# Macaron block (gated FFN, window attention, gated FFN): order of the transposes on SP's queue, tokens' split in the first and last blocks, last quarter with hidden units on the partitions

## The chip, the cores and the metric

The kernel runs on one core of a Trainium2 chip. The time is the device time of one execution in microseconds (us); lower is better. Shown are the median of several runs and one profiled execution.

## What is computed

The input x has 8 sequences of 512 tokens with 512 features. Three stages follow each other, each on a layer norm of x and added to x:

```python
x = x + 0.5 * ffn(layernorm(x), w_gate_up, w_proj)
x = x + attention(layernorm(x), Wq, Wk, Wv, Wo)     # 32 heads of 16, window 128
x = x + 0.5 * ffn(layernorm(x), w_gate_up, w_proj)

def ffn(x, w_gate_up, w_proj):                      # hidden width 2048
    gate, up = split(x @ ternary(w_gate_up).T)
    h = silu(gate) * up
    return (h * rsqrt(mean(h * h) + eps)) @ ternary(w_proj).T
```

The ternary weights are made once, at the start: each group of 64 weights becomes -s, 0 or s. In the attention a query sees the keys of its own block of 128 tokens and of the block before it, masked to a distance of at most 128.

## The kernel before

**Tiling.** The 4096 tokens are 32 blocks of 128. Four blocks are a sequence, so the first block of every fourth has no keys before it. A block goes through stream A (first FFN), B (attention) and C (second FFN). An FFN is done in four quarters of 512 hidden units: a gate product and an up product (`up`, line 1054, eight matmuls of 512 columns each), the gating on ScalarE and VectorE (`hid`), a split of the hidden values into an fp16 high and low part (`hh`), a DMA transpose of both parts (`ht`, `hidden_t`, line 449) and a down product of eight matmuls (`down`, line 1100) that adds to a PSUM bank over the four quarters. ScalarE's Square with an accumulator gives each quarter's sum of squares; GpSimd makes 1/rms of them (`root_mean_square`, line 567), and `add_ffn` (line 905) adds the scaled bank to the block. Tokens are normalised (`norm_stats` on VectorE, line 849; `norm_apply` on GpSimd, line 547) into `xhat`, split into high (ScalarE, line 739) and low (GpSimd, line 592) parts `xh`, and transposed by DMA into `xt`. Queries, keys and probabilities are split and transposed in the same way (`qt`, `kt`, `pt`); so is the attention's output (`ot`).

**Order.** All engines walk through the same list of steps, eight per block, and each engine's function `step_of(step)` holds what it does in a step, in written order. Nothing is scheduled dynamically; semaphores connect the engines. Constants place a stage of block b at step 8b + offset: A's quarters at 0 to 3, B's tokens are split at 7, queries, keys and values are projected at 8, 10 and 12, scores run in groups of four heads at 12 to 19, the products with the values two steps later, the output tokens are split at 21, the output projection is at 22, C's tokens are split at 26 and C's quarters run at 28 to 31. So in the middle every step holds an attention group of one block and an FFN quarter of another. In blocks 2 and 3 of A, and in the fourth and third last of C, the quarters are spread over more steps.

**SP's queue** (lines 462 to 520) issues all transfers one after the other and waits in that order. In a step: queries, then keys (a part of four head pairs, then one of twelve, which the scores need two steps later than the first), tokens of B, of the last block of C, of C, of A, output tokens, the probabilities' high and low parts, and last the units:

```python
                s, b, c = ffn_at(step)
                if s:
                    hidden_t(s, b, c, place(step))
                b = complete("C", step, 4)
                if b is not None:
                    sp.wait_ge(d_x3, b + 1)
                    sp.dma_start(of[b * P:(b + 1) * P, :], slot(b)).then_inc(x_out, 16)
```

Behind it come a finished block's store and, at most every eighth step, the load of a new one (`load_x`). TensorE's order in a step is: gate product, scores of two groups (every other step), the down product of two steps before, a product with the values, the up product, then one of the four projections (lines 1202 to 1295).

**The last block** (31) has a written-out path, since its output projection runs at step 271 (`LAST_WO`) in front of the rest: VectorE normalises it and takes the low part (lines 1035 to 1045), ScalarE copies the high part (line 707) and SP transposes it (line 481) in step 272 (`LAST_SPLIT`). Its quarters of C are steps 276 to 279. In its first steps (lines 1114 to 1178) the kernel transposes the raw weights on TensorE in fp32 (`turn`, line 1130) and has a down product of 128 columns a matmul (`down_first`, line 1163).

Of the kernel before, what the change touches and what calls it, by code (L numbers as in the profile page):

```python
# [24 lines left out]
def macaron(nc, x, Wq, Wk, Wv, Wo, w_gate_up, w_proj, out):  # L25
# [52 lines left out]
    LAST_SPLIT = LAST_WO + 1  # L78

    with ExitStack() as ctx:  # L80
# [33 lines left out]
        hid = sb("hid", [P, 2, CH], F32)  # L114
        squares = sb("squares", [P, 2, CH], BF16)
# [67 lines left out]
        h_first = v_flat[:, 0:4096].bitcast(F32).rearrange("p (c d) -> p c d", c=NC)  # L183
        ps_raw = [ps_s, ps_yy]
# [62 lines left out]
        d_hl = {s: sem(f"d_hl_{s}") for s in "AC"}  # L247
        g_sqp = {s: sem(f"g_sqp_{s}") for s in "AC"}
# [12 lines left out]
        NCONST = 10  # L261
# [64 lines left out]

        def projected(step):

            return ps_m if ffn_at(step)[0] else ps_u

# [75 lines left out]
        def _(sp):  # L406
# [55 lines left out]
            for step in range(FIRST_STEP, STEPS + 2):  # L462
                b = block_at(step, Q_AT + 1)
# [5 lines left out]
                b = block_at(step, K_AT + 1)  # L469
                if b is not None:  # L470
                    sp.wait_ge(a_k, b + 1)
                    sp.wait_ge(d_k, b + 1)
                    need(sp, p_s, 16 * (b - 2))
                    for part, pairs in enumerate((slice(0, 4), slice(4, HEADS // 2))):
                        transpose(kt[:, pairs, b % BPS, :],
                                  k4[:, 2 * pairs.start:2 * pairs.stop, :, :].rearrange("p a b c -> p (a b c)"),
                                  t_k[part])
# [46 lines left out]
        def _(pool):  # L524
            pool.memset(id32[:, :], 0.0).then_inc(consts, 1)
            pool.memset(mask[:, :], 0.0).then_inc(consts, 1)
            pool.memset(neg_half[:, :], -0.5).then_inc(consts, 1)
            pool.memset(prob_bias[:, :], PROB_LOG2 * math.log(2.0)).then_inc(consts, 1)
            pool.memset(blocks[:, :], 0.0).then_inc(consts, 1)
            pool.wait_ge(consts, 5)  # L530
# [47 lines left out]

            pool.wait_ge(fs_step, 6)
# [8 lines left out]
            def step_of(step):  # L588
# [14 lines left out]
                for s in "AC":  # L603
                    b = complete(s, step, 1)
                    if b is not None:
                        root_mean_square(s, b)

# [4 lines left out]
        def _(act):  # L612
# [54 lines left out]
            def hidden_hi(s, b, c, n, ready):  # L667
# [8 lines left out]
                act.activation(squares[:, n % 2, :], hid[:, n % 2, :], ACT.Square,  # L676
                               accum_out=sq_quarter[s][:, c:c + 1]).then_inc(a_sq[s], 1)
# [4 lines left out]
            def step_of(step):  # L682
# [24 lines left out]
                if step == LAST_SPLIT:  # L707
                    split_free(act, step, "C")
                    copy(xh[:, 0, :], xhat[:, :], d_xh, 1, a_xl)

# [3 lines left out]

                s, b, c, n = gate_at(step)
                if s:
                    tanh_half(s, b, c, n)

# [16 lines left out]
                for s, offset in SPLITS:  # L735
                    b = block_at(step, offset)
                    if b is not None and in_steps(s, b) and not (s == "B" and b == 0):
                        split_free(act, step, s)
                        copy(xh[:, 0, :], xhat[:, :], g_xh[s], b + 1, a_xh[s])
# [19 lines left out]
        def _(dve):  # L759
# [144 lines left out]

            def add_ffn(s, b, done):
# [50 lines left out]
            def step_of(step):  # L956
# [40 lines left out]
                if b is not None and b > 0:  # L997
# [14 lines left out]

                b = complete("A", step, 2)
# [21 lines left out]
                if step == LAST_WO:  # L1035
# [281 lines left out]
```

## Time and profile before

| | us |
|---|---|
| median of 3 runs (2029.28 to 2033.4) | 2030.42 |
| the profiled execution | 2029.52 |
| its span | 2027.6 |
| TensorE busy in the span | 1889.7 (93%) |
| VectorE busy | 1555.3 (77%) |
| ScalarE busy | 1499.2 (74%) |
| GpSimd busy | 576.8 (28%) |

The rows further down are of this execution. PE is TensorE, PEld its weight loads, DVE VectorE, ACT ScalarE, POOL GpSimd, and SPq the issue of a DMA by SyncE; L1103 is line 1103 of the kernel. A row of a timeline has the start in us, the length in us, the engine, the line, the operation, what is written and read, the tile's shapes, how often (x8: eight in a row, put together), and in brackets how long the engine sat idle before it and what released it. A row of the table by stretch has the stretch, its length and then busy time (and count) of PE, PEld, DVE, ACT and POOL, the granted clock of TensorE as a share of full speed, the mean share in which the core's 16 DMA engines were busy, and GB/s; a table of a single line has the columns PE and PEld alone. A wait row has engine, tile and line that waited, for what, the sum in us, how many times, and the longest. Matmuls are pipelined, so the lengths of single ones overlap.

### The profile page before, as it was taken

The numbers are of one execution on the slowest core, as the hardware profiler recorded it, in microseconds if no ns is written. First come the engines' busy times: TensorE is split into PE (matmuls) and PEld (weight loads), VectorE is DVE, ScalarE is ACT, GpSimd is POOL, SyncE is SP. The second block draws the span as 40 slices with busy tenths as digits, with TensorE's granted clock in tenths as the row PEclk, the third lists the DMA queues.
The fourth block names the chain that finished last, engine by engine and source line by source line (L and its number), as shares of the span: only waits on it lengthen the run. The fifth ranks groups of instructions, "written<-read, shape, count | busy, mean of one in ns | idle before, by whom it ended". The sixth has DMA issues, their size and how long they took to land. (4 is left out here: it accounts for less than half of the span.)

```text
span 2027.6 us, 37731 instructions
## 1 busy us (share of the span) xinstructions
PE 1889.7 (93%) x12447; PEld 913.0 (45%) x12688; DVE 1555.3 (77%) x4079; ACT 1499.2 (74%) x2871; POOL 576.8 (28%) x559
## 2 busy tenths in 40 slices
PE   6677799999999999999999999999999999999777
PEld 3353344444444444444444444444444444444333
DVE  8966787778787888778787878777887878777763
ACT  7836777777876877777876777777777787777762
POOL 2011333322332333222333332233333232222210
PEclk8888999999999999999999999999999999999989
DMA  7334788778986898878886898788887888878862
GB/s 234 121 64 94 140 150 160 135 138 157 156 153 121 146 163 150 141 143 154 156 143 130 149 161 152 142 142 151 158 145 129 150 157 154 146 128 148 140 116 62
DMA packets 1032673, 287.83 MB, mean 142 GB/s; under 512 B 1017120, under 2 KB 1018144, under 8 KB 1031968
## 3 DMA queue, kind: packets, MB, share of 16 engines
q1 hardware_dynamic: 1032480, 285.41, 77.1%
q8 instruction: 102, 1.67, 0.3%
q14 instruction: 91, 0.75, 0.1%
HBM read 25.17 MB, written 8.39 MB: 17 GB/s over the span
## 5 line engine op out<-in xcount | busy, mean ns | idle before, releaser
L731 ACT ACTIVATE masked<-masked,exp_bias,exp_scale 128x256 f32<-128x256 f32 (+1 forms) x1024 | 503.7, 562 | 8.6
L1103 PE MATMUL ps_yy<-wp_t,ht 128*128 128x512 bf16 x1991 | 479.9, 383 | 28.1 <-DMA ht<-hh 26.7
L1058 PE MATMUL ps_gu<-wgu_t,xt_A 128*128 128x512 bf16 x1941 | 469.0, 383 | 16.6 <-DMA xt_A<-xh 3.7
L1058 PE MATMUL ps_gu<-wgu_t,xt_C 128*128 128x512 bf16 x1944 | 463.1, 380 | 11.5 <-DMA xt_C<-xh 3.5
L860 DVE TENSOR_TENSOR prob<-masked,prob 128x1024 f16<-128x1024 f32 (+1 forms) x256 | 287.2, 1122 | 48.0 <-ACT prob L749 47.7
L1103 PEld LDWEIGHTS ps_yy<-wp_t,ht 128*128 128x128 f16 x2016 | 187.6, 98 | 264.9 <-issue 31.9
L554 POOL TENSOR_TENSOR xh<-xhat,xh 128x512 f16<-128x512 f32 x94 | 109.0, 1160 | 691.9 <-ACT xh L615 691.9
L1058 PEld LDWEIGHTS ps_gu<-wgu_t,xt_A 128*128 128x128 f16 x2048 | 192.1, 98 | 230.1 <-issue 11.7
L1058 PEld LDWEIGHTS ps_gu<-wgu_t,xt_C 128*128 128x128 f16 x2048 | 190.7, 97 | 219.9 <-issue 3.9
L875 DVE SCALAR_TENSOR_TENSOR hid<-ps_gu,h_scale_u,hid 128x512 f32<-128x512 f32 x252 | 189.1, 751 | 121.2 <-PE ps_gu L1058 118.4
L615 ACT ACTIVATE hh<-hid 128x512 f16<-128x512 f32 x256 | 160.6, 627 | 152.5 <-DVE hid L875 145.3
L749 ACT ACTIVATE prob<-masked 128x1024 f16<-128x1024 f32 (+1 forms) x256 | 241.2, 942 | 4.2
L869 DVE SCALAR_TENSOR_TENSOR hid<-hid,ps_gu 128x512 f32<-128x512 f32 x256 | 175.1, 684 | 80.6 <-ACT hid L619 80.6
L619 ACT ACTIVATE hid<-ps_gu 128x512 f32<-128x512 f32 x256 | 150.0, 586 | 116.5 <-PE ps_gu L1058 116.2
L726 ACT ACTIVATE exp_bias<-row_max,prob_bias,neg_exp_scale 128x4 f32<-128x4 f32 x256 | 98.2, 384 | 170.0 <-DVE row_max L886 170.0
L860 DVE TENSOR_TENSOR hh<-hid,hh 128x512 f16<-128x512 f32 x256 | 177.7, 694 | 16.1 <-ACT hh L615 15.7
L886 DVE CUSTOM_DVE_ANT_0 masked<-ps_s,mask 128x256 f32<-128x256 f32 (+1 forms) x512 | 168.7, 385 | 9.8 <-PE ps_s L1093 8.2
L676 ACT ACTIVATE squares<-hid 128x512 bf16<-128x512 f32 x256 | 156.9, 613 | 0.0
L1115 PEld LDWEIGHTS ps_om<-v,pt 128*128 128x128 f16 x3584 | 126.4, 96 | 63.9 <-issue 7.3
L1115 PE MATMUL ps_om<-v,pt 128*128 128x33 f16 x3584 | 129.8, 177 | 3.4 <-DMA pt<-prob 3.0
L896 DVE TENSOR_REDUCE o_sum<-ps_om 128x128 f32<-128x256 f32 x128 | 54.2, 424 | 94.9 <-PE ps_om L1115 94.9
L545 POOL TENSOR_TENSOR rstd_B<-var_eps_B,neg_half 128x1 f32<-128x1 f32 x32 | 17.5, 548 | 353.7 <-DVE var_eps_B L855 353.7
(165 smaller groups left out, 2261.6 us busy)
## 6 DMA issues: line engine op xcount, KB each, us to landing
stream<-in_L_attn_x_dram SPq DMA_DIRECT2D x32, 256.0 KB, 3.3
pt<-prob SPq DMA_TRANSPOSE x512, 3.3
out_dram<-stream SPq DMA_DIRECT2D x32, 256.0 KB, 2.4
prob<-in_L_ffn_w_gate_up_dram SPq DMA_DIRECT2D x4, 1024.0 KB, 5.5
ht<-hh SPq DMA_TRANSPOSE x256, 3.2
stream<-in_L_ffn_w_gate_up_dram SPq DMA_DIRECT2D x3, 1024.0 KB, 5.4
stream<-in_L_ffn_w_proj_dram SPq DMA_DIRECT2D x2, 1024.0 KB, 5.2
prob<-in_L_ffn_w_proj_dram SPq DMA_DIRECT2D x2, 1024.0 KB, 4.8
```

The lines of the kernel that those rows point to most:

```text
L615: act.activation(dst, src, ACT.Copy, scale=scale).then_inc(done, 1)
L619: act.activation(hid[:, n % 2, :], ps_g[:, :], ACT.Tanh, scale=0.5 * 2.0 ** -XS_LOG2).then_inc(a_tanh[s], 1)
L676: act.activation(squares[:, n % 2, :], hid[:, n % 2, :], ACT.Square, accum_out=sq_quarter[s][:, c:c + 1]).then_inc(a_sq[s], 1)
L731: t = act.activation(p, p, ACT.Exp, bias=exp_bias[:, 4 * g + h:4 * g + h + 1], scale=exp_scale[:, 0:1])
L749: act.activation(prob_part(prob[:, g % 2, 0, :, :, :], b), prob_f32(b, g), ACT.Copy).then_inc(a_ph, 1)
L860: dve.tensor_tensor(out=dst, in0=src, in1=hi, op=ALU.subtract).then_inc(done, 1)
L869: dve.scalar_tensor_tensor(out=hid[:, n % 2, :], in0=hid[:, n % 2, :], scalar=1.0, in1=ps_g[:, :], op0=ALU.add, op1=ALU.mult).then_inc(d_g ...
L875: dve.scalar_tensor_tensor(out=dst, in0=ps_u[:, :], scalar=scale, in1=hid[:, n % 2, :], op0=ALU.mult, op1=ALU.mult).then_inc(d_h[s], 1)
L886: m = dve.tensor_tensor_reduce(masked[:, g % 2, 2 * pair + o, first:2 * P], ps_sc[g % 2][o][:, pair * 2 * P + first:(pair + 1) * 2 * P], m ...
L1058: t = pe.matmul(bank[:, :], xt[s][:, part, k, :], wgu_t[:, k, at:at + CH], start=(k == 0 and part == 0), stop=(k == KD - 1 and part == 1))
L1103: t = pe.matmul(ps_y[:, :], ht[:, n % HRING, i, :], wp_t[:, 4 * c + i % 4, :], start=(c == 0 and i == 0), stop=(c == NC - 1 and i == 2 * N ...
L1115: t = pe.matmul(ps_o[:, at:at + VW], pt[:, g % 2, part, half, 2 * pair + o, :], v[:, at_block - 1 + half, hd, 0:VW], start=(n == 0), stop= ...
```

## The change

1. On SP's queue the units' transpose of a step moves from its end to the start of the next step. In a step with keys it stands behind the keys' first part and ahead of the second; the queries' transpose comes after both. It is thereby also behind the store and the load of its own step.
2. In "light" steps (below 32 and from 248 on) ScalarE copies the tokens' high part ahead of the gate's tanh and the exponentials, and VectorE takes B's statistics a step earlier, right behind the addition of A.
3. The last block's split moves from step 272 into 271, on VectorE ahead of the addition, of the hidden values and of their low part, on SP ahead of the units' transpose of step 271.
4. The last quarter of the last block is computed with hidden units on the partitions: weights and tokens change places in the gate and up products, so that `hh` is already what the down product needs and no transpose is made. The sum of squares then goes over partitions: a matmul of the fp32 squares with a column of ones, added to the other three quarters' sum, which GpSimd makes beforehand.

```diff
+        def light(step):
+            return step < 8 * 4 or step >= 8 * LAST
...
             for step in range(FIRST_STEP, STEPS + 2):
+                b = block_at(step, K_AT + 1)
+                if b is not None:
+                    sp.wait_ge(a_k, b + 1)
+                    sp.wait_ge(d_k, b + 1)
+                    need(sp, p_s, 16 * (b - 2))
+                    keys_t(b, 0)
+                s, b, c = ffn_at(step - 1)
+                if s and not is_last(s, b, c):
+                    hidden_t(s, b, c, place(step - 1))
+                b = block_at(step, K_AT + 1)
+                if b is not None:
+                    keys_t(b, 1)
                 b = block_at(step, Q_AT + 1)
...
-                b = block_at(step, K_AT + 1)
-                if b is not None:
...
-                if step == LAST_SPLIT:
+                if step == LAST_WO:
                     sp.wait_ge(d_xl, 1)
                     sp.wait_ge(p_up["C"], 8 * LAST)
...
-                s, b, c = ffn_at(step)
-                if s:
-                    hidden_t(s, b, c, place(step))
                 b = complete("C", step, 4)
...
+            def partial_mean_square():
+                pool.wait_ge(a_sq["C"], 4 * LAST + 3)
...
+                if complete("C", step, 1) == LAST:
+                    power(rms_inv["C"], sq_mean["C"], d_sq, g_rms["C"], 0)
...
+                if is_last(s, b, c):
+                    act.wait_ge(d_pl, 8 * NB)
+                    act.activation(last_squares[:, :], hid[:, n % 2, :], ACT.Square).then_inc(a_sq[s], 1)
...
+                if light(step):
+                    tokens_hi()
                 s, b, c, n = gate_at(step)
                 if s:
                     tanh_half(s, b, c, n)
+                if step == LAST_WO:
+                    split_free(act, step, "C")
+                    copy(xh[:, 0, :], xhat[:, :], d_xh, 1, a_xl)
...
+            def last_mean_square():
+                dve.wait_ge(p_sq, 1)
+                dve.wait_ge(g_part, 1)
+                dve.tensor_scalar(sq_mean["C"][:, :], ps_sq, 4.0 / H, sq_pair["C"][:, 1:2], ALU.mult,
+                                  ALU.add).then_inc(d_sq, 1)
...
                 b = block_at(step, LN_B)
-                if b is not None and b > 0:
+                if b is not None and not light(step):
                     norm_stats("B", b, d_x1, b + 1)
...
                 b = complete("A", step, 2)
                 if b is not None:
                     add_ffn("A", b, d_x1)
+                b = block_at(step, LN_B - 1)
+                if b is not None and b > 0 and light(step):
+                    norm_stats("B", b, d_x1, b + 1)
                 b = complete("C", step, 2)
+                if b == LAST:
+                    last_mean_square()
...
+            def up_by_units(s, c, half, bank):
+                for j in range(4):
+                    at = half * H + (4 * c + j) * P
+                    for k in range(KD):
+                        for part in (0, 1):
+                            t = pe.matmul(bank[:, j * P:(j + 1) * P], wgu_t[:, k, at:at + P], xt[s][:, part, k, :],
+                                          start=(k == 0 and part == 0), stop=(k == KD - 1 and part == 1))
+                t.then_inc(p_up[s], 1)
+
+            def down_by_units(s, b, c, n):
+                for part, ready in ((0, a_hh[s]), (1, d_hl[s])):
+                    pe.wait_ge(ready, 4 * b + c + 1)
+                    for j in range(4):
+                        t = pe.matmul(ps_y[:, :], hh[:, n % 2, part, j * P:(j + 1) * P], wp_t[:, 4 * c + j, :],
+                                      start=False, stop=(part == 1 and j == 3))
+                t.then_inc(p_dn[s], 1)
+                pe.wait_ge(a_sq[s], 4 * b + c + 1)
+                for j in range(4):
+                    t = pe.matmul(ps_sq, last_squares[:, j * P:(j + 1) * P], ones[:, :], start=(j == 0), stop=(j == 3))
+                t.then_inc(p_sq, 1)
```

## Rows read from the trace of the kernel before

**Rows 1.** The table by stretch (columns: see the reading notes above)

```profile
160.00:190.00 30.00, 20.07 (x110) 8.34 (x110) 16.02 (x55) 17.66 (x40) 6.07 (x8) 0.77 0.46 89
...
290.00:1850.00 1560.00, 1537.07 (x10208) 733.89 (x10409) 1229.18 (x3359) 1200.49 (x2364) 494.20 (x460) 1.00 0.83 147
1850.00:1970.00 120.00, 91.94 (x699) 44.01 (x710) 84.54 (x242) 86.61 (x161) 20.11 (x22) 0.94 0.80 138
```

**Rows 2.** The timeline of TensorE at the head (columns: see above)

```profile
163.77 3.01 PE L1058 MATMUL ps_gu<-wgu_t,xt_A 128*128 128x512 bf16 x8 [2.94 <-DMA xt_A<-xh]
...
179.08 5.30 PE L1083 MATMUL ps_gu<-wq,xt_B 128*128 128x512 f16 x12 [3.85 <-DMA xt_B<-xh]
```

**Rows 3.** The waits of TensorE, 290 to 1850 us: total, times, longest

```profile
PE ps_s L1093 <- DMA kt<-k: 9.6, 20, 1.2
```

**Rows 4.** The timeline of SP's queue in one block of the middle

```profile
940.54 1.27 SPq L412 DMA_TRANSPOSE ht<-hh  x1
941.92 2.79 SPq L412 DMA_TRANSPOSE kt<-k  x2
...
947.87 1.29 SPq L412 DMA_TRANSPOSE ht<-hh  x1
949.22 0.57 SPq L512 DMA_DIRECT2D out_dram<-stream  x1
949.88 0.39 SPq L409 DMA_DIRECT2D stream<-in_L_attn_x_dram  x1
```

**Rows 5.** The timeline of TensorE in the same block

```profile
944.51 0.39 PE L1093 MATMUL ps_s<-kt,qt 48*128 48x256 f16 x4 [0.24 <-DMA kt<-k]
...
945.05 1.90 PE L1103 MATMUL ps_yy<-wp_t,ht 128*128 128x512 bf16 x8
...
953.23 1.89 PE L1103 MATMUL ps_yy<-wp_t,ht 128*128 128x512 bf16 x8
```

**Rows 6.** From issue to landing, 290 to 1850 us: of ht, then xt_A

```profile
DMA to landing us min/median/max: 3.0/3.3/5.2
...
DMA to landing us min/median/max: 3.2/3.6/4.2
```

**Rows 7.** The timeline of ScalarE, then of VectorE, at the head

```profile
158.64 0.61 ACT L615 ACTIVATE xh<-xhat 128x512 f16<-128x512 f32 x1
...
169.55 0.69 DVE L851 BATCH_NORM_STATS2 st_B<-stream 128x6 f32<-128x512 f32 x1
```

**Rows 8.** The timeline of TensorE in the last blocks

```profile
1871.44 1.67 PE L1103 MATMUL ps_yy<-wp_t,ht 128*128 128x512 bf16 x7 [1.76 <-DMA ht<-hh]
...
1916.65 0.39 PE L1093 MATMUL ps_s<-kt,qt 48*128 48x256 f16 x4 [2.92 <-DMA kt<-k]
...
1963.67 3.35 PE L1058 MATMUL ps_gu<-wgu_t,xt_C 128*128 128x512 bf16 x8 [2.22 <-DMA xt_C<-xh]
...
1994.40 3.35 PE L1103 MATMUL ps_yy<-wp_t,ht 128*128 128x512 bf16 x8 [3.90 <-DMA ht<-hh]
```

**Rows 9.** The timeline of SP's queue in the last blocks

```profile
1914.02 1.20 SPq L412 DMA_TRANSPOSE kt<-k  x1
...
1992.46 1.29 SPq L412 DMA_TRANSPOSE xt_C<-xh  x1
```

**Rows 10.** The timeline of all engines at the end

```profile
2017.20 0.69 DVE L860 TENSOR_TENSOR hh<-hid,hh 128x512 f16<-128x512 f32 x1 [0.76 <-ACT hh L615]
...
2018.77 0.55 POOL L545 TENSOR_TENSOR rms_inv_C<-sq_mean_C,neg_half 128x1 f32<-128x1 f32 x1
...
2021.01 3.38 PE L1103 MATMUL ps_yy<-wp_t,ht 128*128 128x512 bf16 x8 [3.28 <-DMA ht<-hh]
...
2024.43 0.75 DVE L908 SCALAR_TENSOR_TENSOR stream<-ps_yy,rms_inv_C,stream 128x512 f32<-128x512 f32 x1 [6.54 <-PE ps_yy L1103]
```

**Rows 11.** Line 1169 by stretch; fp32 transposes of line 1130, min/median/max ns

```profile
113.30:117.10 3.80, 3.80 (x71) 3.75 (x68) 1.00 0.00 0
...
L1130 PE MATMUL ps_s<-id,stream x48: 272/273/445, 4.5 to 80.3; 128*128 128x128 f32 x48
```

More of the change, by code:

```diff
@@ L462, in _, with keys_t @@
             for step in range(FIRST_STEP, STEPS + 2):
+                def keys_t(b, part):
+                    pairs = (slice(0, 4), slice(4, HEADS // 2))[part]
+                    transpose(kt[:, pairs, b % BPS, :],
+                              k4[:, 2 * pairs.start:2 * pairs.stop, :, :].rearrange("p a b c -> p (a b c)"), t_k[part])
+                b = block_at(step, K_AT + 1)
[10 more added lines that the diff above has]
+                    keys_t(b, 1)
                 b = block_at(step, Q_AT + 1)
@@ L577, in root_mean_square @@
                 power(rms_inv[s], sq_mean[s], g_sqm[s], g_rms[s], b)
+            def partial_mean_square():
+                pool.wait_ge(a_sq["C"], 4 * LAST + 3)
+                pool.tensor_tensor(out=sq_pair["C"][:, 0:1], in0=sq_quarter["C"][:, 0:1], in1=sq_quarter["C"][:, 1:2],
+                                   op=ALU.add).then_inc(g_sqp["C"], 1)
+                pool.wait_ge(g_sqp["C"], LAST + 1)
+                pool.tensor_tensor(out=sq_sum["C"][:, :], in0=sq_pair["C"][:, 0:1], in1=sq_quarter["C"][:, 2:3],
+                                   op=ALU.add).then_inc(g_sqs["C"], 1)
+                pool.wait_ge(g_sqs["C"], LAST + 1)
+                pool.tensor_scalar(sq_pair["C"][:, 1:2], sq_sum["C"][:, :], 4.0 / H, rms_eps[:, 0:1], ALU.mult,
+                                   ALU.add).then_inc(g_part, 1)
             pool.wait_ge(fs_step, 6)
@@ L604, in step_of @@
                     b = complete(s, step, 1)
-                    if b is not None:
+                    if b is not None and not (s == "C" and b == LAST):
                         root_mean_square(s, b)
+                if complete("C", step, 0) == LAST:
+                    partial_mean_square()
+                if complete("C", step, 1) == LAST:
+                    power(rms_inv["C"], sq_mean["C"], d_sq, g_rms["C"], 0)
             for step in range(FIRST_STEP, STEPS):
@@ L713, in output_hi, with tokens_hi @@
                     copy(oh[:, 0, :], o_norm[:, :], d_on, 4 * b + 4, a_oh)
+                def tokens_hi():
+                    for s, offset in SPLITS:
+                        b = block_at(step, offset)
+                        if b is not None and in_steps(s, b) and not (s == "B" and b == 0):
+                            split_free(act, step, s)
+                            copy(xh[:, 0, :], xhat[:, :], g_xh[s], b + 1, a_xh[s])
+                if light(step):
+                    tokens_hi()
                 s, b, c, n = gate_at(step)
@@ L733, in step_of @@
                     t.then_inc(a_exp, 1)
[L735 to L739, printed above, removed]
+                if not light(step):
+                    tokens_hi()
                 b = block_at(step, SPLIT_O)
@@ L1011, in step_of @@
                         attention_weight(n)
+                if step == LAST_WO:
+                    dve.wait_ge(g_rstd["C"], NB)
+                    xhat_free(dve, step)
+                    dve.tensor_scalar(xhat[:, :], slot(LAST), mean_var["C"][:, 0:1], rstd["C"][:, 0:1],
+                                      ALU.subtract, ALU.mult).then_inc(d_xh, 1)
+                if step == LAST_WO:
+                    take_lo(xh[:, 1, :], xhat[:, :], xh[:, 0, :], a_xl, 1, d_xl)
                 b = complete("A", step, 2)
@@ L1217, in step_of @@
                         pe.wait_ge(d_gate[sb_], 4 * bb + cb + 1)
-                    up(s, c, 0, ps_g)
+                    (up_by_units if is_last(s, b, c) else up)(s, c, 0, ps_g)
                 b, g = group_at(step, SCORES)
@@ L1240, in step_of @@
                         pe.wait_ge(d_x1 if s0 == "A" else d_x3, b0 + 1)
-                    down(s, b, c, place(step - 2))
+                    (down_by_units if is_last(s, b, c) else down)(s, b, c, place(step - 2))
                 b, g = group_at(step, PV)
@@ L1260, in step_of @@
                         projections_taken(step - 1)
-                    up(s, c, 1, ps_u)
+                    (up_by_units if is_last(s, b, c) else up)(s, c, 1, ps_u)
                 for n in weight_halves(step, 0):
```

34 lines of the change are left out of this document (12 added, 22 removed).

## The prediction

> **What bounds the kernel now.** I read the profile in three stretches, because the change touches three places. First the table by stretch: from 290 to 1850 us TensorE is busy 1537.1 of 1560 us at the full clock, so there only an idle moment of TensorE is worth anything; from 160 to 190 it is busy 20.1 of 30 at a mean clock of 0.77, and from 1850 to 1970 91.9 of 120 at 0.94 [rows 1]. Then what TensorE waited for. At the head two waits for tokens stand out, 2.94 us for those of the gate product of step 14 and 3.85 us for those of the query projection of step 16; that projection then took 5.30 us for 12 matmuls [rows 2]. At the full clock a matmul of 512 columns takes 0.217 us (8 in 1.90 us [rows 5], the last one's own 0.38 off, over 7), so 12 take 2.8. In the middle one wait alone counts: the scores wait for the keys' transpose, 20 times, 9.6 us in all [rows 3]. In the last steps the waits are for the units' transpose (1.76 us), the keys' (2.92 us) and tokens (2.22 us), and behind the last attention group 3.90 us for units again [rows 8]. Last the end itself: 3.28 us of waiting for one transpose, then eight matmuls in 3.38 us, the addition, the store [rows 10]. The profiled execution took 2029.5 us for a span of 2027.6 us; its runs' median is 2030.4, 0.9 above, and I add that at the end.
>
> **Keys' transpose ahead of the units' (26 blocks of the middle, steps 35 to 235).** SP issues everything in one order. In a typical block the units' transpose of step 8b+10 is issued at 940.54 and the keys' two at 941.92; scores begin at 944.51 after 0.24 us of waiting, and the down product that reads those units follows at 945.05 [rows 4, 5]. SP itself is the late one there, since keys and units were both ready while it issued the transposes before. With the new order the keys' first part goes out at 940.54 and its wait is gone. The units go out one issue later, 1.2 us and a gap of 0.1: at 941.85. Units land 3.3 us after issue in the median, 3.0 at least, 5.2 at most [rows 6]: at 945.15. The down product could now start at 944.81, starts at 945.15 and did start at 945.05. So the wait moves from the keys to the units: +0.1 per block at 3.3, -0.15 at 3.1, +0.4 at 3.6. About 19 of the 26 blocks look like this one, the others have some 0.4 us to spare. Sum of the term: 0.2, from -2.6 to +7. The scores themselves come 0.24 us sooner; nobody waits for that in the middle.
>
> **Units' transpose behind the store and the load.** Because the units' transpose of a step is now issued at the start of the next, that of step 8b+11 goes behind the output's store and the next input's load: 0.57 + 0.39 and two gaps of 0.09, so 1.14 us later, 949.01 instead of 947.87 [rows 4]. It lands at 952.3, its down product began at 953.23 [rows 5]: hidden, with 0.9 to spare. Over the blocks I find between 0.1 and 1.5 us to spare; at 3.3 us of latency the tightest blocks lose 0.5 us together. What stands directly behind a load today is the tokens' transpose of stream A, and it lands after 3.6 us, 4.2 at most [rows 6]; with 3.6 the term is 1.7. The Trainium skill has a rule against this part (DMA: Bandwidth & Descriptors, Queues, rings and completion order): a transfer's completion is signalled only after all earlier writes of the same DMA engine, so a small transpose can't report ahead of the load in front of it. The trace agrees in direction: 3.6 behind a load, 3.3 else. By the rule this term is the 1.7, without it 0.5. I take 0.5 and keep 1.7 for the range.
>
> **Tokens and statistics sooner in the first blocks (steps below 32).** At step 12 ScalarE copies the high part of the tokens at 158.64, behind the exponentials [rows 7]; it was idle and the tokens ready at 155.7, so they come 3.0 us sooner and the 2.94 us wait goes [rows 2]. Late next is the transpose of the probabilities of step 13, which I put at 166.3: the gate product starts 2.9 sooner, the products behind it hardly. The larger part is step 15. Block 1's statistics began at 169.55 [rows 7], behind step 14's masking and gate; moved right behind the residual addition they begin at about 162.0. The normalised tokens are then ready at 166.2, the copy waits only for step 14's exponentials, until 167.7, and the transpose lands at 173.6: the query projection starts at 173.7, not 179.08, -5.4 us. If the clock holds it also takes 2.5 less (5.30 - 2.8). Behind it the units' transpose of step 15 is late, landing at about 177.5 in place of 183.5, -6.6 at the next down product. From this I take off 1.1: TensorE still idles 2.8 us near 165, and behind such an idle time the gate product's eight matmuls now take 3.01 us [rows 2], 1.1 more than 1.90. **What the earlier statistics delay:** statistics, aggregate and scale (about 1.0 us on VectorE) now stand ahead of the output tokens' low part in steps 21, 29 and 253, and that feeds the output projection. For step 21 I come to +1.0 with the later units' transpose of step 19. At step 27 the keys come ahead of units whose place the tokens blocked: -1.0. Sum of the head -5.5; -2 if only the first wait goes and the rest is taken back, -9 if the clock recovers as well.
>
> **The same in the last blocks (steps from 248).** Three places. (a) Steps 250 to 255: the probabilities' transposes no longer queue behind the tokens', so the units land 1.8 sooner and the 1.76 us wait goes [rows 8]; the statistics ahead of the output tokens take back 0.9; block 31's tokens, a step earlier in their statistics, give 1.1. Sum -2.0. (b) Steps 258 to 261: the keys went out at 1914.02 behind tokens, probabilities and units; they can go at 1910.5. Of the 2.92 us wait at the scores [rows 8, 9] the down product keeps 0.7, but here VectorE and ScalarE, not TensorE, carry the chain from the scores to the values, so -2.9. (c) Step 266: tokens at 1960.0 in place of 1963.6, wait of 2.22 us gone, then the units' transpose, 2.1 sooner, decides: -2.4. Sum -7.3, from -3 to -9.
>
> **Last block's tokens ahead of its units (step 271).** TensorE's order is unchanged: the down product of step 273 waits for units until 1994.40 and ends at 1997.7. The tokens were issued at 1992.46 and in place at 1995.7 [rows 8, 9]. Hidden before, hidden after: 0. They could delay the units by one issue, 1.2, but their last wait ends at 1988.8, when the units aren't ready yet: 0.
>
> **Last quarter with units on the partitions.** The up product becomes 2 x 32 matmuls of 128 columns instead of 2 x 8 of 512. Such matmuls exist in the first block's down product: 68 weight loads in 3.80 us, 56 ns each at the full clock [rows 11], so 1.79 per half against 1.73: +0.1. Now: low part at 2017.20 for 0.69, transpose, down product from 2021.01 for 3.38, addition at 2024.43 [rows 10]. After: the high half of the down product (4 x 0.217) behind the previous product, 2017.5 to 2018.4; the low half to 2019.3. The sums of squares come now from four fp32 matmuls of one column. Nearest row: fp32 transposes of 128 columns, 0.27 us each [rows 11]; four in a row between 0.4 and 1.1, I take 0.7: 2020.0. Then a VectorE instruction on one column 0.25, the power on GpSimd 0.55 as now [rows 10] with two hand-overs of 0.1, the addition at 2021.3 instead of 2024.43, with 0.1 for the first item already in. Term -3.1, from -2.3 to -3.6.
>
> **Sum:** 0.2 + 0.5 - 5.5 - 7.3 - 3.1 = -15.2; 2029.5 - 15.2 = 2014.3, and with the 0.9 of the median 2015.2.
>
> **Rivals.** (1) *The middle gives it back.* The units' transposes land at 3.6 or later: +8.7 in the middle in place of 0.7, 2023. For it: the slack is 0.1 us per block and DMA engines are busy 83% of the stretch [rows 1]; against it: the median is 3.3 [rows 6]. (2) *The head only shifts its waits.* Probabilities and the clock decide there, and the head gives 2 and the last steps 4: 2022. For it: the head's 0.77 of clock. (3) *Better:* units land at 3.1 behind the short keys' part and the head's clock recovers: -2.5 and -3 more, 2009. (4) *Slower, by one mechanism:* the store and load in front of the units' transpose of step 8b+11. If it lands later than 4.2 us after issue, the 5.36 us between 947.87 and 953.23 less the 1.14 are used up, and TensorE waits in all 26 blocks. The other terms bring 15.7, so it decides from 4.2 + 0.75 = 4.95 us on; at 5.2, the worst landing of rows 6, the loss is 26 and the time 2041. Against it: 4.2 is the most behind a load today. (5) *It doesn't do what it says:* the edges' waits are all replaced by others, the middle loses 2: 2029.
>
> **Chances.** Forecast 0.56 (2010 to 2020), rival 1 0.15, rival 2 0.13, rival 3 0.09, rival 5 0.04, rival 4 0.03. 0.2% (4 us) is about what a measurement of this kernel can tell from no change. Range 2008 to 2024: it takes in rivals 1 to 3 nearly whole. Faster 0.92, within 0.2% 0.05, slower 0.03.
>
> **What would show it.** Waits for the keys near zero in the middle and in their place some 20 short waits for units; TensorE's busy time in 290 to 1850 within 2 us of now. The query projection of step 16 starts near 173.7 and takes under 3 us. The last scores wait (step 260) is gone. After the last up product no transpose, and 5.5 us from there to the addition's start. I am wrong if the middle has grown by more than 5 us, if step 16's projection starts later than 177, or if the four fp32 matmuls take over 1.5 us.

## The result and the profile after

The changed kernel takes 2040.3 us in the median of 20 runs (2031.98 to 2046.02), the kernel before 2032.52 (2028.0 to 2036.78, 20 runs): ratio 1.0038, 95% interval 1.0028 to 1.0048. It is slower, by 7.8 us; forecast was 2015.2, range 2008 to 2024. The profiled execution took 2036.8 us for a span of 2034.7 us, 7.1 more than before's span.

To see where it went I took each down product's first weight load in both traces and subtracted. A step's number is that of its quarter; the down product follows two steps later. After minus before, in us:

| down product of | after | what lies in front |
|---|---|---|
| step 34 | -6.8 | head |
| step 247 | +13.3 | middle, +20.1 |
| step 271 | +10.3 | last blocks, -3.0 |
| step 278 | +10.2 | last split and last quarters, -0.1 |
| end of the span | +7.1 | last quarter's end, -3.1 |

So head, last blocks and end gained 13.0 us together, and the middle took 20.1.

The table by stretch, of the kernel after (columns as in [rows 1]):

```profile
160.00:190.00 30.00, 23.39 (x152) 10.46 (x151) 20.41 (x78) 21.93 (x50) 6.12 (x5) 0.94 0.54 98
...
290.00:1850.00 1560.00, 1532.98 (x10271) 722.70 (x10270) 1213.14 (x3324) 1185.03 (x2332) 483.37 (x456) 1.00 0.83 145
1850.00:1970.00 120.00, 100.66 (x748) 47.03 (x746) 89.47 (x260) 90.37 (x167) 24.87 (x22) 0.94 0.82 142
```

The head's clock rose from 0.77 to 0.94, in the middle it is 1.00 as before [rows 1]. TensorE's busy time in the middle fell by only 4 us although 20 us of work left the stretch: some of before's matmul records are missing. For the same work between the down products of steps 34 and 247 there are 10005 of them before and 10204 after, and idle times under 0.1 us add up to 11.4 us before and 0.2 after. So this row can't be the measure I had wanted it to be. The waits can. TensorE's waits between 290 and 1850 us, after:

```profile
PE ps_yy L1177 <- DMA ht<-hh: 22.8, 33, 2.0
PE ps_om L1157 <- issue: 2.3, 4, 0.9
PE ps_s L1167 <- DMA kt<-k: 1.0, 3, 0.4
PE ps_om L1157 <- DMA xt_B<-xh: 0.7, 1, 0.7
```

The keys' 9.6 us [rows 3] are down to 1.0, as forecast; the units' waits stand at 22.8 us, and they were 0.9 before (3 of them). These two account for 13.3 of the 20.1 us. All waits of the view together are 11.2 us before and 26.8 after, which makes 15.6. Two more things are in the starts and in no wait row. In step 8b+11 the last matmul in front of the wait is shown 0.16 us beyond where the next one would start, so that its wait row is that much short of the loss, in 12 blocks some 2 us. And in one block the clock fell behind the longest of these waits, first the down product, then the table by stretch:

```profile
1064.37 2.56 PE L1177 MATMUL ps_yy<-wp_t,ht 128*128 128x512 bf16 x8 [1.98 <-DMA ht<-hh]
```

```profile
1064.00:1067.00 3.00, 2.63 (x17) 1.20 (x17) 1.26 (x9) 2.92 (x7) 0.48 (x1) 0.74 1.15 246
1067.00:1070.00 3.00, 3.00 (x24) 1.29 (x21) 0.00 (x0) 0.00 (x0) 1.85 (x5) 0.69 1.07 286
```

The granted clock was 0.74 and 0.69 in these two stretches, and the matmuls behind the wait took 1.5 us longer than the same ones before. That makes 19 of the 20 us.

One block of the middle shows how it goes, first SP's queue, then TensorE, the block of [rows 4, 5]:

```profile
942.30 1.21 SPq L423 DMA_TRANSPOSE kt<-k  x1
943.61 1.26 SPq L423 DMA_TRANSPOSE ht<-hh  x1
944.92 1.56 SPq L423 DMA_TRANSPOSE kt<-k  x1
```

```profile
945.94 0.39 PE L1167 MATMUL ps_s<-kt,qt 48*128 48x256 f16 x4
...
946.93 1.90 PE L1177 MATMUL ps_yy<-wp_t,ht 128*128 128x512 bf16 x8 [0.38 <-DMA ht<-hh]
```

The scores wait for nothing now; the units go out 1.31 us behind the keys and land 3.3 us later, and the down product waits 0.38 us for them. For step 8b+11, SP and then TensorE in another block:

```profile
719.47 0.57 SPq L528 DMA_DIRECT2D out_dram<-stream  x1
720.14 0.39 SPq L420 DMA_DIRECT2D stream<-in_L_attn_x_dram  x1
720.63 1.23 SPq L423 DMA_TRANSPOSE ht<-hh  x1
...
724.57 1.69 PE L1177 MATMUL ps_yy<-wp_t,ht 128*128 128x512 bf16 x7 [0.35 <-DMA ht<-hh]
```

Behind the store and the load the transpose takes 3.9 us to land, and the down product starts right then. Before, the units of this step were there 1.5 us before the down product's first weight load.

The end of the kernel after, TensorE, VectorE and GpSimd, for [rows 10]:

```profile
2026.01 0.75 DVE L916 SCALAR_TENSOR_TENSOR hid<-ps_gu,h_scale_u,hid 128x512 f32<-128x512 f32 x1 [2.01 <-PE ps_gu L1120]
...
2027.76 1.89 PE L1128 MATMUL ps_yy<-wp_t,hh 128*128 128x512 bf16 x8
...
2029.48 0.95 PE L1133 MATMUL ps_om<-ones,masked 128*128 128x1 f32 x8
2030.47 0.22 DVE L949 TENSOR_SCALAR sq_mean_C<-ps_om,sq_pair_C 128x1 f32<-128x1 f32 x1 [2.27 <-PE ps_om L1133]
2030.77 0.55 POOL L562 TENSOR_TENSOR rms_inv_C<-sq_mean_C,neg_half 128x1 f32<-128x1 f32 x1 [7.07 <-DVE sq_mean_C L949]
2031.42 0.75 DVE L955 SCALAR_TENSOR_TENSOR stream<-ps_yy,rms_inv_C,stream 128x512 f32<-128x512 f32 x1 [0.74 <-POOL rms_inv_C L562]
```

No transpose is left behind the last gated units; from there to the addition it is 5.41 us.

### The profile page after: what moved, and what is told of

Its sections match the earlier page's. It is cut to its first block, busy times and chain, and to the rows that moved or that the text cites. A ratio compares the mean times of both kernels' runs of the same rounds, so it can differ in the third digit from the quotient of the medians.

```text
span 2034.7 us, 38085 instructions
## 1 busy us (share of the span) xinstructions
PE 1907.7 (94%) x12744; PEld 915.7 (45%) x12744; DVE 1554.3 (76%) x4080; ACT 1501.4 (74%) x2870; POOL 574.3 (28%) x560
## 4 chain that ended last, share of the span: by engine, by line
PE 56%; SPq 11%; DMA 7%; DVE 5%; ACT 4%; issue 4%; POOL 1%; DVEq 0%; ACTq 0%; POOLq 0%
PE ps_gu L1111 26%; PE ps_yy L1177 15%; SPq L423 10%; PE ps_om L1157 10%; DMA ht<-hh 6%; PE ps_om L1189 3%; ACT masked L775 2%; DVE masked L927 2%; DVE prob L901 2%; POOL xh L571 1%; PE ps_s L1167 1%; ACT xh L647 1%; ACT exp_bias L770 1%; PE ps_yy L1167 1%; DVE hid L916 1%
## 5 line engine op out<-in xcount | busy, mean ns | idle before, releaser
L1111 PE MATMUL ps_gu<-wgu_t,xt_A 128*128 128x512 bf16 x2048 | 482.1, 381 | 3.0 <-DVE hid L910 2.5
L1111 PE MATMUL ps_gu<-wgu_t,xt_C 128*128 128x512 bf16 x2032 | 474.5, 379 | 1.8 <-DVE v L905 1.2
```

The costliest lines, as they stand in the source:

```text
L1111: t = pe.matmul(bank[:, :], xt[s][:, part, k, :], wgu_t[:, k, at:at + CH], start=(k == 0 and part == 0), stop=(k == KD - 1 and part == 1))
```

## Experiments

**Which part of the change costs the time?** First the changed kernel with SP's queue in the old order, then the kernel before with the new order alone.

```diff
-                s, b, c = ffn_at(step - 1)
-                if s and not is_last(s, b, c):
-                    hidden_t(s, b, c, place(step - 1))
...
+                s, b, c = ffn_at(step)
+                if s and not is_last(s, b, c):
+                    hidden_t(s, b, c, place(step))
                 b = complete("C", step, 4)
```

> The changed kernel with SP's order as before (keys behind the units, units at the end of their own step, ahead of store and load); tokens, statistics, last split and last quarter stay changed. Theory A (the loss of 19.7 us between 306 and 1850 us is SP's order alone: the units' transpose of step 8b+10 behind the keys' first part, 8.9 us, and that of step 8b+11 behind store and load, 11.1 us): 19.7 of the changed kernel's 2040.3 come back, some 3 of the edges' gain go (keys sooner at steps 27 and 259), so 2020 to 2025, and the waits for units in the middle are again under 2 us. Theory B (the token copies, statistics or the last quarter cause it): 2036 to 2042.

Measured: 2018.44 us (2017.42 to 2020.34, 5 runs), ratio 0.9922 (0.991 to 0.9934) against before: 22 us faster than the changed kernel, and below the 2020 to 2025 of theory A, because the edges gave nothing back. Its waits between 290 and 1850 us are those of before:

```profile
PE ps_s L1167 <- DMA kt<-k: 10.7, 20, 1.3
PE ps_om L1157 <- issue: 1.8, 4, 1.1
PE ps_yy L1177 <- DMA ht<-hh: 0.8, 3, 0.4
```

For the new order alone, the same lines are moved the other way in the kernel before (keys' first part, units of the step before, keys' second part, then queries).

> The kernel before with the new order of SP's queue and nothing else of the change. Theory A: 2032.5 plus 19.7 less some 3 at the edges, 2047 to 2052. Theory B: within 4 us of before.

Measured: 2053.71 us (2047.71 to 2056.55, 6 runs), ratio 1.0087 (1.0072 to 1.0102), theory A with 2 us over its range. The new order costs about 20 us with or without the other parts (19.8 and 21.9 by the medians). In its trace the units' wait is 25.1 us in the middle, the keys' 0.3.

**Which of the two places?** Two more kernels on the changed one: units of every step but the keys' back ahead of the store and load, with the keys first as changed; and units ahead of both parts of the keys, still behind store and load.

```diff
                 s, b, c = ffn_at(step - 1)
-                if s and not is_last(s, b, c):
+                if s and not is_last(s, b, c) and block_at(step, K_AT + 1) is not None:
                     hidden_t(s, b, c, place(step - 1))
...
+                s, b, c = ffn_at(step)
+                if s and not is_last(s, b, c) and block_at(step + 1, K_AT + 1) is None:
+                    hidden_t(s, b, c, place(step))
                 b = complete("C", step, 4)
```

> The changed kernel, but units' transposes go ahead of the store and the load of their step; only in a step before one with keys does it stay behind the keys' first part. Theory A, with two separate losses: 11 us come back, 2029; units of step 8b+11 land 3.2 us after issue again instead of 3.9 in the median. Theory C (one loss feeds the other, because a late start of the down product moves everything behind it): either part alone costs nearly all, 2036 or more here.

```diff
+                s, b, c = ffn_at(step - 1)
+                if s and not is_last(s, b, c):
+                    hidden_t(s, b, c, place(step - 1))
                 b = block_at(step, K_AT + 1)
...
                     keys_t(b, 0)
-                s, b, c = ffn_at(step - 1)
-                if s and not is_last(s, b, c):
-                    hidden_t(s, b, c, place(step - 1))
```

> The changed kernel, but units' transposes are issued ahead of both parts of the keys; they stay at the start of the next step, behind store and load. Theory A: the 8.9 us of step 8b+10 come back, the edges lose some 3, so 2034; the waits for units at step 8b+11 stay, 15 or so. Theory C: 2036 or more.

Measured: 2028.55 us (0.9966, 0.9952 to 0.9979) and 2027.44 us (0.9969, 0.9957 to 0.9981). Each undoes about half, the first as forecast (2029), the second by more than forecast (2034). The growth of the middle between the down products of steps 34 and 247, and what the down products of steps 8b+10 and 8b+11 alone add to it (27 blocks each, from first matmul to first matmul), us:

| kernel | 8b+10 | 8b+11 | middle |
|---|---|---|---|
| changed | +8.9 | +8.4 | +20.1 |
| SP's old order | +1.1 | 0.0 | +2.4 |
| new order alone | +9.1 | +9.7 | +19.3 |
| keys first, units ahead of store | +9.9 | +1.5 | +12.2 |
| units ahead of keys, behind store | +0.3 | +5.6 | +8.3 |

The 11.1 us that the expectations have for step 8b+11 is the same loss taken at the first weight load. Before, that load runs 0.21 us ahead of its matmul; where TensorE waited for the units, load and matmul start together, and in the next step 2.8 us come back. The matmuls themselves start 8.4 us later.

The two losses are separate and add up, theory A: over the old order's +2.4 the single parts grow by 9.8 and 5.9, both together by 17.7. What the two columns leave of the middle is 0.6 to 2.8 us in all kernels of the table, in those with the old order too. Eight kernels with the old order in the middle show +1.5 to +4.4 in their traces, so a difference of 3 us here says nothing.

**What in front of the transpose makes it late, store or load?** On the kernel with the old order, the units go between the store and the load, or behind a load that goes ahead of the store.

```diff
-                s, b, c = ffn_at(step)
-                if s and not is_last(s, b, c):
-                    hidden_t(s, b, c, place(step))
                 b = complete("C", step, 4)
                 if b is not None:
                     sp.wait_ge(d_x3, b + 1)
                     sp.dma_start(of[b * P:(b + 1) * P, :], slot(b)).then_inc(x_out, 16)
+                s, b, c = ffn_at(step)
+                if s and not is_last(s, b, c):
+                    hidden_t(s, b, c, place(step))
                 b = block_at(step, LN_A - 7)
```

> SP's old order, but the units' transpose of step 8b+11 between the store and the load. Theory D (the load in front of it makes a transpose land late): issued 0.66 us later, lands 3.2 us after issue, costs 1 us at most, 2019. Theory E (only the moment of issue counts, each 0.1 us about alike): 0.66 of the 1.14 us, half of the 11 us, 2024.

> SP's old order, but the units' transpose of step 8b+11 behind the load, and the store behind it. Theory D: issued 0.47 us later and landing 3.9 to 4.1 us after issue, 4 to 7 us slower than with the old order, 2023 to 2025. Theory E: 2021 at most, landings at 3.2.

Measured: 2020.16 us (0.9937, 0.9924 to 0.995) and 2023.12 us (0.9947, 0.9933 to 0.996). The times are theory D's, but the intervals of the two overlap, and behind the load the median landing is 3.55, not the 3.9 to 4.1 that theory D asked for. From the start of the issue on SP's queue to landing, units of the 27 steps 8b+11, worked out from each trace's issues and landings:

| in front of the units' transpose | median us | mean us | over 3.6 |
|---|---|---|---|
| probabilities (before) | 3.15 | 3.52 | 7 of 27 |
| store | 3.38 | 3.76 | 11 of 27 |
| load | 3.55 | 3.96 | 13 of 27 |
| store and load (changed) | 3.94 | 4.07 | 21 of 27 |
| store and load (new order alone) | 4.04 | 4.19 | 20 of 27 |
| store and load (units ahead of keys) | 3.69 | 4.01 | 17 of 27 |

The ten kernels with neither in front have means of 3.50 to 3.59, so each adds something, and both together 0.5 to 0.6 us. That the load adds more than the store isn't shown: block by block the difference is 0.20 us with a standard error of 0.10. Late landings alone don't cost much either: with only the store or only the load in front the units go out 0.5 to 0.7 us later, and steps 8b+11 lose 1.2 and 2.1 us, against 8.4 with both. The second kernel's middle grew by 8.6 in its trace, 3.6 of it at steps 8b+10, whose place on the queue it doesn't change; the cause of that stays open. The Trainium skill's rule (DMA: Bandwidth & Descriptors, Queues, rings and completion order), that a transfer isn't reported ahead of earlier writes of its DMA engine, agrees in direction; that it is the cause, rather than the engines being shared, no run here shows.

**What are the light steps worth?** The old-order kernel without them (`light` returns False), and with only the early copies (B's statistics back in their step).

```diff
-            return step < 8 * 4 or step >= 8 * LAST
+            return False
...
```

> The changed kernel with SP's old order and without light steps: tokens' high part and block statistics where they were. By the traces the light steps give 7 at the head and some 4 in the last blocks, so 2029. If the gain of SP's old order were there anyway: under 2022.

```diff
-                if b is not None and not light(step):
+                if b is not None and b > 0:
                     norm_stats("B", b, d_x1, b + 1)
...
-                b = block_at(step, LN_B - 1)
-                if b is not None and b > 0 and light(step):
-                    norm_stats("B", b, d_x1, b + 1)
```

> SP's queue in the old order; tokens' copies early in the light steps, but stream B's statistics back in their old step; last quarter by units kept. Theory S (the prediction's): the earlier statistics are the larger half of the light steps' 13 us, since they pull the query projection of step 16 from about 177 to 173.7: the head gives back 4 to 6 us and keeps 2 to 3, 2023 to 2026 us. Theory T: the early copies do most, because the earlier statistics delay the output tokens (steps 21, 29 and 253) by about what they gain elsewhere: within 2 us of the changed kernel with SP's old order, 2017 to 2020.

Measured: without light steps 2032.08 us (11 runs, 0.9993, 0.9984 to 1.0001), so they are worth 13.6 us (forecast 11). In the traces it is 7.7 at step 34 (-7.1 with, +0.6 without) and 5.8 from step 247 to 271 (-4.6 and +1.2). With the copies alone 2023.24 us (0.9949, 0.9937 to 0.9962): the statistics are worth 4.8 of the 13.6. The time is theory S's, but its place isn't. TensorE at step 16 with the copies alone, then in the changed kernel:

```profile
174.59 4.35 PE L1154 MATMUL ps_gu<-wq,xt_B 128*128 128x512 f16 x12 [4.08 <-DMA xt_B<-xh]
```

```profile
173.94 4.45 PE L1157 MATMUL ps_gu<-wq,xt_B 128*128 128x512 f16 x12 [3.06 <-DMA xt_B<-xh]
```

It was 179.08 before [rows 2], and it is 174.23 in the kernel with SP's old order and both parts: the copies bring 4.5 of the 5.1 us there. The statistics pay a block later. From step 19 to 23 the kernel with them gains 1.5, the one without loses 0.6. At step 34 the head has gained 7.1 us with both and 3.6 with the copies alone.

**Do keys first pay at least in the first and last blocks?**

```diff
+                s, b, c = ffn_at(step - 1)
+                if s and not is_last(s, b, c) and block_at(step, K_AT + 1) is not None and light(step):
+                    hidden_t(s, b, c, place(step - 1))
...
                 s, b, c = ffn_at(step)
-                if s and not is_last(s, b, c):
+                if s and not is_last(s, b, c) and not (block_at(step + 1, K_AT + 1) is not None and light(step + 1)):
                     hidden_t(s, b, c, place(step))
```

> Old order of SP's queue in the middle; only in the light steps (first and last blocks) do the keys' first part go ahead of the units' transpose of the step before; light steps and last quarter by units kept. Theory P (the prediction's term b): the keys' first part ahead of tokens, probabilities and units is worth up to 2.9 us at the scores of step 260: 2014 to 2016 us. Theory Q: the wait of step 260 is already cut by the tokens' earlier copies, the comparison of step 258 to 266 between the changed kernel and the one with the old order gave 0.3 us for it: 2017.5 to 2019.5.

Measured: 2018.17 us (0.9926, 0.9912 to 0.994) against 2018.44 without it: nothing, theory Q.

**The last split and the last quarter.** Each taken out of the old-order kernel, then the light steps alone, and once more light steps with the last quarter by units.

```diff
-                if step == LAST_WO:
+                if step == LAST_SPLIT:
                     split_free(act, step, "C")
                     copy(xh[:, 0, :], xhat[:, :], d_xh, 1, a_xl)
...
```

> SP's queue in the old order, light steps and last quarter by units kept; the last block's split back in step 272. The prediction costs this part at nothing, as its tokens were in place 2 us before they are read: 2018.4 within 1 us, and the down product of step 278 within 0.3 us of where it starts with the split in step 271. Rival: TensorE's product of step 276 or 277 waits for it, 1 to 3 us more.

```diff
         def is_last(s, b, c):
 
-            return s == "C" and b == LAST and c == NC - 1
+            return False
...
```

> The last run with SP's old order, and the last quarter as before too (tokens on the partitions, transpose, sum of squares by ScalarE's accumulator). If that part is worth the 3.1 us of the prediction: 2018.4 + 3.1 = 2021.5. If the four fp32 matmuls of one column take as much as the transpose: 2018 to 2019.

> The light steps alone: SP's queue in the old order, the last block's split back in step 272, the last quarter with tokens on the partitions and its transpose. Theory U (last quarter by units is worth its 3.2 us in the runs as in the trace, where the stretch from the last gated units to the addition is 5.4 us with it and 8.7 without): 2019 to 2021 us, 3 above the same kernel with that part, 2016.4 before. Theory V (it is worth nothing in the runs, as two medians of 2018.44 with and without it let one think): within 1 us of the same kernel with it.

> The kernel with the last split as before once more (light steps and last quarter by units, SP's old order), beside the light steps alone on one chip: 2016.4 within 1.5 us. Theory U: 3 us below the light steps alone; theory V: the same as those.

| kernel (SP's old order, light steps) | us | ratio, interval | span of its trace |
|---|---|---|---|
| split moved, last quarter by units | 2018.44 | 0.9922, 0.991 to 0.9934 | 2016.3 |
| split moved, transposed | 2018.44 | 0.9928, 0.9915 to 0.9941 | 2019.4 |
| split as before, by units | 2016.38 | 0.9918, 0.9904 to 0.9931 | 2012.8 |
| the same again | 2015.94 | 0.992, 0.9905 to 0.9935 | 2015.2 |
| split as before, transposed | 2018.42 | 0.9933, 0.9918 to 0.9948 | 2016.2 |

The split's place is worth nothing that these runs can tell: the medians with the split as before are 2.1 and 2.5 us lower, where within 1 us was forecast, but the ratios are the same within 0.0004. In the traces it is nothing, as the prediction said: with the split as before, the down products of steps 271 and 278 stand at -11.7 and -11.7, in the changed kernel at +10.3 and +10.2. The last quarter is 3.2 us shorter in the traces; where it is transposed the end reads (VectorE, TensorE, VectorE):

```profile
2007.53 0.75 DVE L912 SCALAR_TENSOR_TENSOR hid<-ps_gu,h_scale_u,hid 128x512 f32<-128x512 f32 x1 [1.89 <-PE ps_gu L1105]
...
2012.86 3.30 PE L1171 MATMUL ps_yy<-wp_t,ht 128*128 128x512 bf16 x8 [3.29 <-DMA ht<-hh]
2016.20 0.75 DVE L951 SCALAR_TENSOR_TENSOR stream<-ps_yy,rms_inv_C,stream 128x512 f32<-128x512 f32 x1 [6.46 <-PE ps_yy L1171]
```

That is 8.67 us from the gated units to the addition, against 5.41 with it. In the runs one pair shows 0 and the other 2.5 us, and the intervals overlap in both. So the trace shows the 3.2 us, the runs only that the part doesn't harm.

The kernel with SP's old order, the light steps and the last quarter by units beats both: 2016 us, 16 below before and 24 below the changed kernel.

## Why the prediction was wrong

The sum came to -15.2 us, the spans show +7.1. Of the 22.3 between them, 19.4 are the middle (+20.1 for the 0.7 of the first two terms), 4.3 the last blocks, and -1.3 the head.

**Keys ahead of the units: right place, wrong size.** The keys' waits went, and short waits for units came, as written. The sum said 0.2, and the down products of steps 8b+10 lost 8.9. The step that failed is "Units land 3.3 us after issue in the median", used for all blocks. TensorE starts now when the units land: in 22 of 27 blocks the slack between landing and down product is 0.04 us. With no slack, it is the mean that counts, not the median. The five blocks whose units landed after 3.8 to 4.9 us lost 6.0 us together. The 22 others, all within 3.5 us, lost 2.9, and 1.8 of that lies in three where a second input was off: the issue of the keys' first part took 1.8 to 2.2 us there, not "one issue later, 1.2 us". One of them on SP's queue:

```profile
1232.97 2.19 SPq L423 DMA_TRANSPOSE kt<-k  x1
1235.26 1.26 SPq L423 DMA_TRANSPOSE ht<-hh  x1
```

In before's trace one keys' issue is that long too. Before, such landings are there as well (up to 4.4 us), and no down product of these steps waited for one: 1.3 us of slack stood behind the landing in the mean. The bound of +7 was nearly right; it stood in the range of a term and had no weight in the sum.

**Units behind store and load: the same step, and once the clock.** The sum said 0.5, with 1.7 kept for the range; steps 8b+11 lost 8.4. The room was read rightly: with before's issues and down products, block by block, and the 1.14 us of store and load, a landing of 3.3 in every block gives the 0.5, and 3.6 the 1.7, if the room ends at the first weight load; up to the first matmul they are 0.2 and 0.7. What failed is again one landing for all blocks, 3.3 or, from stream A's tokens behind a load [rows 6], 3.6. In the changed kernel these units land after 3.1 to 6.1 us, 3.9 in the median and 4.1 in the mean, so the tokens' row wasn't the nearest case either. The lowered clock of one block, 1.5 of the 8.4 us, was in no term.

With the landings as they came, block by block and up to the first matmul, the prediction's own arithmetic gives 6.5 for this term and 4.7 for the keys, 11.3 where the sum had 0.7. The 0.04 us from a landing to TensorE's start add 1.5, the three long issues 2.3, the clock 1.5: together 16.6 of the 17.2 us that the two steps lost. So the mechanism was right and the landings that went into it were not. The sign of being wrong that the prediction names, a middle grown by more than 5 us, came up.

Rival 1 named this mechanism and priced it at 8.7 and 2023 us. Rival 4 had the place of one half and the side of the result, and asked for a landing over 4.95 us in all blocks. That was the wrong condition: only three of 27 passed it, and the sum over a spread of landings costs long before the worst one is typical. That its 2041 lies beside the measured 2040.3 is luck.

**Head: right in sum, wrong in cause.** -6.8 for -5.5. The query projection of step 16 starts at 173.94, forecast 173.7, and takes 4.45 us, so the clock recovered only in part there. But the copies, not the statistics, bring most of the 5.1 us at this projection, and half of the head at step 34.

**Last blocks: -3.0 for -7.3.** Of the three places (b) failed most clearly. The scores of step 260 and the down product behind them, after:

```profile
1926.63 0.40 PE L1167 MATMUL ps_s<-kt,qt 48*128 48x256 f16 x4 [0.96 <-DMA kt<-k]
...
1928.55 3.15 PE L1177 MATMUL ps_yy<-wp_t,ht 128*128 128x512 bf16 x8 [1.31 <-DMA ht<-hh]
```

and in front of them VectorE's low part of the keys and SP's queue:

```profile
1923.23 0.69 DVE L905 SCALAR_TENSOR_TENSOR k<-ps_om,k 128x512 f16<-128x512 f32 x1
```

```profile
1921.23 2.60 SPq L423 DMA_TRANSPOSE pt<-prob  x2
1923.99 1.20 SPq L423 DMA_TRANSPOSE kt<-k  x1
1925.31 1.23 SPq L423 DMA_TRANSPOSE ht<-hh  x1
```

The step "they can go at 1910.5" was nearly right. The keys go out as soon as their low part is written, and with the 13.0 us taken off by which that low part is later than before, this is 1911.0: 3.0 us sooner and not 3.5. The scores start 10.0 us behind before, the down product of step 257 in front of them 13.4, so they gained 3.4, of which 1.4 come from the tokens' wait (1.24 us before) that went at the gate product in front. The step that failed is "so -2.9", which let all of the gain pass on: the units behind the keys take 1.31 us back at the down product (the sum had 0.7 and didn't count it), 0.9 us were lost between steps 255 and 257, and from 255 to 258 the gain is 1.2. The comparison with SP's old order (0.9 from 255 to 258) gives the keys' place 0.3 of it. Place (a) came to 0.7 for 2.0. Place (c) came true at step 266, -2.3 for -2.4, but 1.4 us were lost between 258 and 265, and no term of the sum has them. I didn't trace these 1.4. The last blocks vary between kernels with the same order: from step 247 to 271 five kernels with the old order and light steps show -3.1, -3.9, -4.6, -5.0 and -5.6, so I don't read more into them.

**Last split: 0, right. Last quarter: right in its trace.** -3.1 forecast, -3.1 seen between step 278 and the end; the fp32 matmuls took 0.95 us, forecast 0.7.

## What to carry to other kernels

Where a change takes an engine's slack away, price a transfer by the spread of its landings, each against the slack of its block, and never by the median in all blocks: the late fifth cost two thirds of the first loss. Even the mean is too little where some slack is left: 4.07 in every block gives 4.2 us behind store and load, the landings as they came 6.5. A wait of 0.2 to 0.5 us on a short transfer can be the cheaper one to keep, when removing it puts the next transfer an issue later. And read a term's bounds into the sum: a term with a bound of +7 and one with a rival of +26 were entered as 0.2 and 0.5.

## What the runs showed of the hardware

**Landings spread.** The 217 units' transposes that before issues between 290 and 1850 us land 3.27 us after issue in the median, 3.45 in the mean, and a fifth needs over 3.6. For the same stretch the view of the tile says, for the changed kernel, then for the one with SP's old order:

```profile
DMA to landing us min/median/max: 3.0/3.3/6.1
```

```profile
DMA to landing us min/median/max: 3.0/3.3/5.0
```

The medians are the same in two kernels that are 22 us apart; the means are 3.51 and 3.44.

**The same wait costs a different time at the clock.** Behind the last attention group TensorE waits for units, and its clock falls. Clock in stretches of 3 us, in the kernel with the old order and then in the one with the keys first in the light steps:

```profile
1983.00:1986.00 3.00, 0.92 (x3) 0.37 (x4) 0.00 (x0) 0.00 (x0) 0.39 (x1) 0.59 0.46 87
1986.00:1989.00 3.00, 3.00 (x9) 1.07 (x8) 0.28 (x1) 0.00 (x0) 0.00 (x0) 0.50 0.02 5
1989.00:1992.00 3.00, 3.00 (x12) 1.19 (x11) 0.50 (x2) 0.60 (x1) 0.00 (x0) 0.77 0.23 87
1992.00:1995.00 3.00, 3.00 (x15) 1.37 (x14) 1.73 (x3) 0.99 (x2) 0.00 (x0) 1.00 0.00 0
```

```profile
1986.00:1989.00 3.00, 0.44 (x2) 0.17 (x3) 0.00 (x0) 0.00 (x0) 0.80 (x2) 0.85 0.46 87
1989.00:1992.00 3.00, 3.00 (x10) 1.11 (x9) 0.05 (x1) 0.00 (x0) 0.00 (x0) 0.58 0.02 5
1992.00:1995.00 3.00, 3.00 (x16) 1.32 (x14) 1.39 (x2) 0.60 (x1) 0.00 (x0) 1.00 0.23 87
```

0.50 is 1.2 GHz and 1.00 is 2.4 GHz. In the first the lower level reaches over three stretches, in the second mostly over one. The next down product stands 13.45 us behind in the first and 12.31 in the second, with the same work between. All fifteen traces fall on one side or the other (12.2 to 12.6, or 13.3 to 13.8 us), and the two traces of one kernel, light steps with the last quarter by units, on different sides (12.4 and 13.3). So about 1.1 us at this place is no effect of a change.
